# A feed-forward tile's residual, added by an accumulating transfer from GpSimd's queue

## What is computed

```python
x = x + 0.5 * ffn(layernorm(x))     # first feed-forward stage, result called x1
x = x + attention(layernorm(x))     # result called x2
x = x + 0.5 * ffn(layernorm(x))     # second feed-forward stage

def ffn(n):                         # 9 paths, each 256 -> 64 -> 256
    m = mix(n)                      # three-tap mix over neighbouring tokens
    h = einsum('bsd,pdm->bspm', m, W1) + b1
    paths = einsum('bspm,pmd->bspd', h, W2) + b2
    scores = tanh(m @ Wo1 + bo1) @ Wo2 + bo2
    chosen = paths[argmax(scores)]  # by a one-hot weight per token
    return layernorm(n + chosen) * gamma + beta
```

## Time and profile before

| what | value |
|---|---|
| median of 3 runs | 1463.25 us (1462.21 to 1463.43) |
| span of the profiled execution, first to last instruction | 1460.0 us |
| what the median has around that span | 3.25 us |
| TensorE matmul busy | 1336.2 us, 92% |
| VectorE busy | 1178.4 us, 81% |
| ScalarE busy | 923.2 us, 63% |
| GpSimd busy | 326.0 us, 22% |

### The profile page before, as it was taken

How to read it: one execution, slowest core, us unless ns; L and a number is a source line. 1 busy time by engine, 2 the same in 40 slices (tenths; PEclk the granted TensorE clock), 3 DMA queues, 4 the chain that set the end, 5 groups by cost and what they waited for, 6 DMA issues and landing times.

```text
span 1460.0 us, 24657 instructions
## 1 busy us (share of the span) xinstructions
PE 1336.2 (92%) x7700; PEld 773.8 (53%) x7700; DVE 1178.4 (81%) x2326; ACT 923.2 (63%) x1717; POOL 326.0 (22%) x359
## 2 busy tenths in 40 slices
PE   3999998868999999999879999999998879999995
PEld 2567765644454454544344455454544336777764
DVE  5999998876778777788875787787778768989986
ACT  5676764446567666566866567666575866766641
POOL 2255553432010000040011010000130004555422
PEclk9899999979999999999999999999999989999998
DMA  6243333320001100011201010000002211433321
GB/s 157 51 125 109 113 99 91 92 73 0 16 29 36 38 0 29 1 44 38 79 1 44 30 44 16 29 15 15 29 15 74 86 32 51 121 93 108 92 79 58
DMA packets 86985, 82.18 MB, mean 56 GB/s; under 512 B 8539, under 2 KB 86884, under 8 KB 86884
## 3 DMA queue, kind: packets, MB, share of 16 engines
q1 hardware_dynamic: 86884, 80.91, 18.4%
HBM read 55.43 MB, written 25.46 MB: 55 GB/s over the span
## 4 chain that ended last, share of the span: by engine, by line
PE 64%; DVE 15%; issue 9%; ACT 8%; POOL 2%; DMA 1%; DVEq 0%; ACTq 0%; POOLq 0%; SPq 0%
PE PS L1618 57%; DVE R L1047 2%; PE PS L1626 2%; DVE R L1041 2%; PE PS L1716 2%; ACT R L1458 2%; ACT R L1462 2%; DVE run_max L1035 1%; PE PS L1687 1%; DVE x_st L1069 1%; ACT R L1417 1%; POOL R L608 1%; DVE R L852 1%; DVE st L751 1%; DMA R<-in_L_attn_x 1%
## 5 line engine op out<-in xcount | busy, mean ns | idle before, releaser
L1618 PE MATMUL PS<-R 128*128 128x512 f16 (+3 forms) x3456 | 718.4, 362 | 36.1 <-DVE R L1047 29.7
L1618 PEld LDWEIGHTS PS<-R 128*128 128x128 f16 (+1 forms) x3456 | 325.9, 98 | 395.6 <-DVE R L1047 58.8
L1047 DVE TENSOR_TENSOR R<-R 128x512 f16<-128x512 f32 (+3 forms) x288 | 188.7, 655 | 96.1 <-ACT R L1462 94.4
L1449 ACT ACTIVATE R<-PS 128x512 f32 (+5 forms) x288 | 160.3, 558 | 158.8 <-PE PS L1618 158.8
L1458 ACT ACTIVATE R<-R 128x512 f32<-128x512 f32 (+4 forms) x288 | 169.6, 589 | 52.2 <-DVE R L1041 51.3
L1618 PE MATMUL PS<-R,w_hi 128*128 128x512 f16 x640 | 195.5, 388 | 4.3 <-DVE R L801 4.3
L1618 PE MATMUL PS<-w_hi,R 128*128 128x256 f16 x1024 | 189.0, 274 | 10.5 <-DVE R L843 10.5
L1462 ACT ACTIVATE R<-R 128x512 f16<-128x512 f32 (+3 forms) x288 | 171.1, 594 | 26.7 <-ACT R L1458 0.4
L1041 DVE TENSOR_TENSOR R<-R,max_row 128x512 f32<-128x512 f32 (+4 forms) x288 | 186.8, 648 | 0.5 <-ACT max_row L1526 0.5
L1035 DVE TENSOR_TENSOR run_max<-run_max,R 128x512 f32<-128x512 f32 (+3 forms) x272 | 175.6, 645 | 8.4 <-DVE run_max L1035 1.7
L575 POOL TENSOR_SCALAR veps<-mv 128x4 f32<-128x4 f32 x48 | 16.4, 343 | 653.4 <-issue 376.0
(11 more groups left out here) (124 smaller groups left out, 1752.5 us busy)
## 6 DMA issues: line engine op xcount, KB each, us to landing
R<-x_scratch SPq DMA_DIRECT2D x48, 512.0 KB, 4.1
x_scratch<-R SPq DMA_DIRECT2D x32, 512.0 KB, 3.2
R<-oh_scratch SPq DMA_DIRECT2D x32, 320.0 KB
R<-in_L_attn_x SPq DMA_DIRECT2D x16, 512.0 KB, 5.1
R<-oh_scratch SPq DMA_DIRECT2D x32, 256.0 KB
out<-R SPq DMA_DIRECT2D x16, 512.0 KB, 3.2
R<-in_L_ffn_W SPq DMA_DIRECT2D x2, 288.0 KB
R<-in_L_ffn_W SPq DMA_DIRECT2D x1, 512.0 KB
```

Source lines behind the costliest of these rows:

```text
L1047: v.tensor_tensor(p_lo[:, i * TT + lo:(i + 1) * TT], pf[:, (i % 2) * TT + lo:(i % 2 + 1) * TT], p_hi[:, i * TT + lo:(i + 1) * TT], ALU.sub ...
L1449: a.activation(cols(ring, ring_m + i * TT + lo, TT - lo), ps_s[:, i, lo:], ACT.Abs, scale=1.0 / (QS * XS * D ** 0.5)).then_inc(abs_done, 1)
L1618: ins = t_.matmul(dst, w, xx, start=start and n == 0, stop=stop and n == last, skip_group_check=skip)
```

## The change

For all tiles except the last one of the second stage, VectorE no longer adds the residual. GpSimd issues an accumulating transfer from `x_rows` to `n_rows`, both in SBUF, at the end of its turn (behind `norm_scale` or `first_scales`), when the rows are scaled and beta has been added. The transfer counts `x1_done` by 16 when it has landed; each one waits for the one before. SyncE's store and GpSimd's and VectorE's later waits count in sixteens. The last tile of the second stage stays on VectorE, with a semaphore of its own. The sums of the finished tiles 8 to 12 (`added_sums`) are taken one turn later and earlier within the turn, in front of the masks 2 and 3.

```diff
--- before.py
+++ after.py
@@ -212,6 +212,7 @@
         o_psum, y_done, sq_done, r_eps, r_rstd = (sem("o_psum"), sem("y_done"), sem("sq_done"), sem("r_eps"),
                                                   sem("r_rstd"))
         scaled_done, xb_done, x1_done, stored = sem("scaled_done"), sem("xb_done"), sem("x1_done"), sem("stored")
+        last_added = sem("last_added")
 
         a_hi, a_lo, aT_psum, aT_hi, aT_lo = sem("a_hi"), sem("a_lo"), sem("aT_psum"), sem("aT_hi"), sem("aT_lo")
         q_psum, q_hi_done, spare_free = sem("q_psum"), sem("q_hi_done"), [sem("spare_free0"), sem("spare_free1")]
@@ -371,6 +372,10 @@
         def out_banks(t):
 
             return ps_n if t == NTT - 1 else ps_o
+
+        def by_vector(ph, t):
+
+            return ph == 1 and t == NTT - 1
 
         def turns():
             return range(-STATS, NTT + 1)
@@ -468,7 +473,10 @@
 
                 def store(t):
                     g = use(ph, t)
-                    sp.wait_ge(x1_done, g + 1)
+                    if by_vector(ph, t):
+                        sp.wait_ge(last_added, 1)
+                    else:
+                        sp.wait_ge(x1_done, 16 * (g + 1))
                     if g >= 1:
                         sp.wait_ge(stored, 16 * g)
                     sp.dma_start(dram_tile(dst, t), rows4(n_rows(t))).then_inc(stored, 16)
@@ -608,6 +616,15 @@
                     g.tensor_tensor(rows4(x_rows(t)), rows4(x_rows(t)),
                                     beta_b[:, :].unsqueeze(1).to_broadcast([P, SUB, D]), ALU.add).then_inc(xb_done, 1)
 
+                def residual_added(t):
+
+                    k = use(ph, t)
+                    pool.wait_ge(scaled_done, k + 1)
+                    pool.wait_ge(xb_done, k + 1)
+                    if k >= 1:
+                        pool.wait_ge(x1_done, 16 * k)
+                    g.dma_start(n_rows(t), x_rows(t), accum_op=ALU.add).then_inc(x1_done, 16)
+
                 def turn(t):
                     if on(t - 1):
                         result_scale(t - 1)
@@ -621,6 +638,8 @@
                                    (n_var, n_eps, n_rstd, n_neg, n_shift))
                     elif first_of(ph, t):
                         first_scales(0, first_of(ph, t))
+                    if on(t - 1) and not by_vector(ph, t - 1):
+                        residual_added(t - 1)
 
                 for t in turns():
                     turn(t)
@@ -641,7 +660,7 @@
                                     ALU.subtract).then_inc(a_lo, 1)
 
                 if b == 0:
-                    pool.wait_ge(x1_done, NTT)
+                    pool.wait_ge(x1_done, 16 * NTT)
                 for t in range(EARLY):
                     key_low(t)
                 for t in range(EARLY, NT):
@@ -857,11 +876,11 @@
 
                     dve.wait_ge(xb_done, use(ph, t) + 1)
                     dve.wait_ge(scaled_done, use(ph, t) + 1)
-                    v.tensor_tensor(n_rows(t), n_rows(t), x_rows(t), ALU.add).then_inc(x1_done, 1)
+                    v.tensor_tensor(n_rows(t), n_rows(t), x_rows(t), ALU.add).then_inc(last_added, 1)
 
                 def added_sums(t):
 
-                    dve.wait_ge(x1_done, t + 1)
+                    dve.wait_ge(x1_done, 16 * (t + 1))
                     for u in range(SUB):
                         ins = v.bn_stats(sums_at(t, u), cols(n_rows(t), u * D, D))
                     ins.then_inc(x1_sums, 1)
@@ -944,6 +963,8 @@
                     if ph == 0 and rows:
                         for u in range(SUB):
                             input_sum(t + STATS, u)
+                    if ph == 0 and 0 <= t - 2 - NT < EARLY:
+                        added_sums(t - 2)
                     if here:
                         masked(t + HIDDEN, 2)
                         masked(t + HIDDEN, 3)
@@ -962,10 +983,8 @@
                         masked_low(t + HIDDEN, 1)
                         if not whole(ph, LAST):
                             masked_low(t + HIDDEN, 2)
-                    if last:
+                    if last and by_vector(ph, t - 1):
                         result_added(t - 1)
-                        if ph == 0 and 0 <= t - 1 - NT < EARLY:
-                            added_sums(t - 1)
                     if ph == 0 and t == -ROUTE:
                         prepare_second()
                     if ph == 0 and t == FOLD:
```

## The result

| | before | after |
|---|---|---|
| median of the runs shown together | 1462.73 us (1461.53 to 1463.43) | 1479.81 us (1478.42 to 1480.25) |
| span of the profiled execution | 1460.0 us | 1477.9 us |
| ratio after / before | | 1.012, 95% interval 1.0108 to 1.0132 |

The change costs 17.1 us in the medians and 17.9 us in the spans.

What follows compares the result with a forecast made beforehand. TensorE and VectorE were taken as full in the first stage's 15.55 us turns, TensorE as the second stage's limit. 1463.25 us, +48 for late loads, -8 first stage's end, -0.6 second stage: 1502 us, range 1468 to 1561.

Steps and rivals of the forecast that it cites:

- the rival with a short transfer: The accumulating transfer takes only 2.6 to 5 us from GpSimd being ready to landing: 1466 to 1481 us, chance 20%.
- X: Time from GpSimd being ready to issue the transfer until `x1_done` is up, taken as 7 us.
- First stage's end: Turns 9 and 11 to 15, where VectorE's queue sets the next start: relief from adds and sums saves 12 us.
- Second stage: Three turns at its end, with the add directly before a result, give 3.4 us; its loads have slack.
- the loop: First stage, turns 2 to 9: incoming statistics wait for a load behind the transfer; 8 x (X - 1.0) = 48 us.
- the moved sums: First stage: sums moved one turn later wait for the previous turn's accumulation, eating about 4 of 12 us at X = 7.
- the last store: End of second stage: it waits for the store before, which awaits an accumulation; takes X - 4.2 us back.
- TensorE's clock: Rival: stalled turns lower TensorE's granted clock to an assumed 0.67, making its turn 23.2 us: +53, 1516 us, chance 6%.
- Faster: Rival: VectorE's relief in both stages' last turns wins while the load stays on time; needs X below 2.6, chance 4%.
- break-even: Loop cost against relief in both stages' last turns: 8 x (X - 1.0) < 15.4, X below 2.9.

Runs made afterwards that it cites:

- e3: Changed kernel, but the transfer copies instead of accumulating, leaving the normalised result out: 1467.63 us, ratio 1.003 to the kernel before.
- e5: Changed kernel, but GpSimd issues the transfer ahead of norm_scale instead of behind it: 1465.43 us, ratio 1.0016 to the kernel before.
- e1: Changed kernel, but VectorE adds the residual of the first stage's tiles 0 to 7 again: 1447.57 us, ratio 0.989 to the kernel before.

## Why the prediction was wrong

The direction, the place and the mechanism were right; the size was forecast at +39 us and is +17. The measured time lies inside the range, but in the band that was given to the rival with a short transfer (1466 to 1481), 1 us below the forecast's own (1481 to 1533).

**The term that was mis-sized is X**, the time from GpSimd being ready to `x1_done`. The forecast took 7 us, built of a store's landing (3.2), a second pass over the data (1.7) and one long GpSimd instruction (about 2). In the trace it is 0.33 us to the start and, over the eight transfers that count, 4.6 to 6.1 us to landing, 5.0 on average: 5.3 us. The first two parts together, 4.9 us, were right for the landing, and e3 shows them apart: 3.0 for the copy and 1.6 for accumulating. Why single transfers took up to 6.1 us stays open. The third part doesn't exist on top: the issue occupies GpSimd for 0.94 us, but that lies inside the time to landing. The step that failed is the sentence "GpSimd must also prepare it, and its small instructions take 0.2 to 2.3 us": durations of arithmetic that had been held by VectorE were added as the price of issuing. The Trainium skill (SBUF — State Buffer, Who interferes with whom) infers that two SBUF inputs on VectorE don't hold the writing of descriptors. The traces agree: L626 took 924 to 1075 ns in all 31 cases, and 0.95 us in e5 too, where it starts at 141.10 and lies almost wholly beside L929 (140.72 to 141.94). The Trainium skill's fit for a transfer from GpSimd (DMA: Bandwidth & Descriptors, Anatomy of one DMA), an estimate of 3.2 us for 512 KB, is near the copy's 3.0 us; for the accumulation it would be 1.4 us short.

**The sum with X = 5.3**, all else as written: 8 x (5.3 - 1.0) = 34 against eight turns of 15.55; measured, the eight spacings add up to 158.95 us, 34.6 more. But L824 had already waited 1.0 us in the kernel before, which the forecast read and then left out of its sum: against that trace the gap is 33.5. First stage's end: 12 us less a little, measured 13.4. Second stage: 3.4 - 0.8 = 2.6, measured 2.8. Total +19, about 1482; measured 1479.8. Each microsecond of X weighs 8 us and more. The 1.7 us by which X was too long are 14 us in the loop and, by the forecast's own terms, about 4 in the moved sums and 2 at the last store, 20 of the 22 us by which +39 was too much.

**Point by point.** The waits of L843 were forecast at 5 to 6 us each and are 5.1 on average, but the turns grew by 4.2 us, not by 6. The two agree only because the forecast of the waits left something out: the 1.1 us that VectorE was relieved of in each turn turn into waiting as well, 4.2 + 1.1 = 5.3, a little of it spent on TensorE in front of L862 instead. Six results L862 wait for TensorE, 9.1 us in the row of the result section, three of them in the eight turns with 1.2 to 1.4 us each. L592 fell from 2.29 to 1.15 us as forecast (about 1.2). The second stage's turns stayed: its loads are issued at 1298.54 and 1314.08, 15.54 us apart. The moved sums waited for a transfer 2.7 us in all, forecast as about 4 at X = 7. The gain in the last turns of the first stage was taken for 12 and is 13.4 in these two traces; by the medians the sums give more (7.5 instead of 5.3) and the add less (4.3 in e1 instead of 6.8), part of it paid for the sums' waits. At the range's lower end the forecast's own terms give 1467 (8 x 2.4 - 15.4 = 3.8), not 1468; that changes nothing here.

**TensorE's clock**, the fourth rival, did show, but it is not in the loop. TensorE was busy 86% of the eight turns, not 73%: they were shorter than forecast, and where the granted clock was below 1.00 single products took up to 634 ns where the median is 379. The part of the loop that runs through the engines, from the start of L843 to the end of L595, after which the transfer goes out, is 9.10 us at a granted clock of 1.00 (turn of 136.72) and 9.10 us at 0.67 (turn of 156.52):

```profile
L1637 PE MATMUL PS<-R,w_hi x18: 378/379/634, 104.4 to 121.5; 128*128 128x512 f16 x18
```

```profile
136.72:145.82 9.10, 6.78 (x43) 4.80 (x40) 9.10 (x19) 4.67 (x6) 2.72 (x4) 1.00 0.24 67
156.52:165.62 9.10, 5.81 (x19) 3.57 (x18) 8.62 (x18) 4.34 (x6) 2.72 (x4) 0.67 0.23 66
```

The two stretches at 0.84 above end with L862 waiting 1.2 and 1.4 us for TensorE. VectorE then still stands idle for 5.2 and 3.4 us in front of the next load, so these waits move no load.

**The other rivals.** "Faster" needed X below 2.6. The quarter transfer comes closest with 2.7 us to landing and ends at no difference, ratio 1.0001: near the point that the prediction named for break-even (X = 2.9), and with 0.33 us added a little above it.

## What to carry to other kernels

A pass taken off an engine at 99% is worth nothing where another engine is just as full; look for the turns in which its queue stands before the next release, and move it only there: the same transfer costs 4 us a turn where a load waits for its slot and saves 8 us where none does (15.6 with the moved sums, which gave 7.5 by themselves). Before a wait is put on a buffer's release, follow who refills the buffer and who reads the refill; if the reader stands in front of the releaser in the next turn, it is a loop and every microsecond is paid once per turn. And where a price is missing from the trace, add up only what is serial in it: here a store row plus one pass over the data gave 4.9 us for a transfer that takes 4.6, a single case, in which two rows of other transfers happened to fit.

## What the runs showed of the hardware

An accumulating transfer of 512 KB within SBUF, issued by GpSimd, lands 4.6 us after its start (median; up to 6.1), a plain one after 3.0 (up to 5.1); the accumulation occupies the 16 DMA engines 2.2 times as long (5.8% against 2.7% of the span). A quarter of the size lands after 2.7 us. The issue itself takes GpSimd 0.94 us for an accumulation, whether 512 KB or 128 KB, and 0.63 us for a copy. The same 128x4 scaling on GpSimd took 2.29, 1.15, 0.49 and 0.23 us. In the first three cases it started beside a VectorE pass over two SBUF tensors and ended 0.09 us behind the last of such passes (L860 at 131.88, L929 at 145.34, L805 at 143.83); in the fourth it started 0.03 us ahead of one and was not held. That the pass holds it is the reading that fits all four, no run changed it alone.
